# Loads moved to other issuers, repeated products in the last attention steps, and a bias product put last: one change to an attention and feed-forward kernel

## The reference

```python
q = x @ q_w.T + q_b
xd = conv1d(x, conv_w, stride=2, padding=1, groups=C) + conv_b     # 2048 -> 1024 keys
k = xd @ k_w.T + k_b;  v = xd @ v_w.T + v_b
att = softmax(q_heads @ k_heads.T / 4)
y = concat_heads(att @ v_heads) @ out_w.T + out_b
x = layernorm(x + y)
h = layernorm(x) * gamma + beta
w1 = (fc1_q - 128) * scales1;  w2 = (fc2_q - 128) * scales2        # 256 x 1024 and 1024 x 256
z = silu(h @ w1 + fc1_bias) @ w2 + fc2_bias
out = layernorm(x + x + 0.5 * z)
```

## Time and profile of the kernel before

| | us |
|---|---|
| median of 3 runs | 3946.15 |
| lowest, highest | 3940.93, 3949.59 |
| the profiled execution | 3952.87 |
| its span | 3951.1 |

### The profile page before, as it was taken

One profiled execution on the slowest core, in us unless ns is written; L12 is line 12 of the kernel. 1 busy time (PEld: TensorE's weight loads), 2 busy tenths in 40 slices (PEclk: granted clock), 3 DMA queues, 4 the chain that ended last, 5 costly groups with the idle time before them and its releaser, 6 DMA issues. The chain is left out here.

```text
span 3951.1 us, 76505 instructions
## 1 busy us (share of the span) xinstructions
PE 3847.0 (97%) x22696; PEld 1997.0 (51%) x22696; DVE 3336.2 (84%) x4142; ACT 2612.8 (66%) x4968; POOL 840.7 (21%) x547
## 2 busy tenths in 40 slices
PE   9979999999999999999999999999998899999998
PEld 5633333333333333333333333333333799999998
DVE  9968998999899899989989998999995677777775
ACT  4427887878788788878878887878875343343343
POOL 6531000000000000000000000000001687787785
PEclk9979999999999999999999999999997899999999
DMA  8992124105112411510231151133110222222220
GB/s 294 346 207 57 34 38 66 32 29 69 34 33 44 59 34 30 68 37 30 47 56 34 34 70 34 32 50 55 34 56 30 75 86 71 78 85 71 77 85 27
DMA packets 316156, 269.34 MB, mean 68 GB/s; under 512 B 156593, under 2 KB 226225, under 8 KB 316082
## 3 DMA queue, kind: packets, MB, share of 16 engines
q1 hardware_dynamic: 316082, 268.55, 27.9%
HBM read 157.30 MB, written 110.10 MB: 68 GB/s over the span
## 5 line engine op out<-in xcount | busy, mean ns | idle before, releaser
L711 DVE TENSOR_REDUCE half_max<-first_ps 128x2 f32<-128x1024 f32 x2048 | 2413.5, 1221 | 290.8 <-PE first_ps L563 287.1
L679 ACT ACTIVATE probs<-score_ps 128x512 f32<-128x512 f32 x4096 | 2114.9, 603 | 604.0 <-PE score_ps L588 603.4
L588 PE MATMUL score_ps<-q_s,k_s 49*128 49x512 f32 x4096 | 1449.2, 479 | 34.4 <-DMA q_s<-max_row 20.1
L588 PEld LDWEIGHTS score_ps<-q_s,k_s 49*128 49x128 f32 x4096 | 576.7, 186 | 1299.9 <-ACT probs L679 1154.9
L598 PE MATMUL pv_ps<-probs,v_s 128*32 128x512 f32 x8192 | 1109.1, 614 | 0.0
L563 PE MATMUL first_ps<-k_s,q_s 48*128 48x512 f32 x4096 | 912.0, 423 | 26.8 <-PEq L657 18.8
L817 POOL TENSOR_TENSOR num<-num,rden 128x1024 f32<-128x1024 f32 x2 | 4.7, 2356 | 2687.2 <-DMA rden<-rden_d 2687.2
L992 ACT ACTIVATE act_f<-fc_ps,b 128x512 f32<-128x512 f32 x256 | 174.9, 684 | 464.4 <-PE fc_ps L945 462.3
L563 PEld LDWEIGHTS first_ps<-k_s,q_s 48*128 48x128 f32 x4096 | 412.4, 189 | 79.9 <-issue 20.0
L1069 DVE CAST a_hi<-act_f 128x512 fp32r<-128x512 f32 x256 | 243.6, 952 | 146.0 <-ACT act_f L992 144.9
L1121 POOL TENSOR_TENSOR a_lo<-act_f,a_hi 128x512 fp32r<-128x512 f32 x256 | 339.6, 1331 | 86.6 <-DVE a_hi L1069 86.6
(11 more groups left out here) (99 smaller groups left out, 2501.0 us busy)
## 6 DMA issues: line engine op xcount, KB each, us to landing
q_s<-q_hi_d SPq DMA_DIRECT2D x512, 64.0 KB, 2.1
o_d<-o_sb SPq DMA_DIRECT2D x128, 256.0 KB, 2.1
x_t<-x_c_in SPq DMA_DIRECT2D x32, 512.0 KB, 5.7
q_hi_d<-q_hi SPq DMA_DIRECT2D x32, 512.0 KB, 4.7
q_lo_d<-q_lo SPq DMA_DIRECT2D x32, 512.0 KB, 5.1
k_s<-k_hi_d SPq DMA_DIRECT2D x128, 128.0 KB, 4.4
q_s<-q_lo_d SPq DMA_DIRECT2D x256, 64.0 KB, 2.1
x_res<-x_in SPq DMA_DIRECT2D x32, 512.0 KB
```

Of the source, the lines that this page charges most:

```text
L588: pe.matmul(bank(s, u)[:, :], k_s[g][at, a, t * P:(t + 1) * P], q_s[g][at, a, :], start=True, stop=True).then_inc(scored, 1)
L679: nc.scalar.activation(probs[s % 2][:, u, :], bank(s, u)[:, :], ACT.Exp).then_inc(exped, 1)
L711: dve.reduce_max(half_max[g % 2][:, :, a * TT + t, keys], first_ps[keys][:, :, :], AX.X)\
```

## The change

The three loads of each feed-forward weight move to GpSimd's queue: the first behind a wait for the last score of block 0 of attention, the second behind GpSimd's work on the first. SyncE keeps group 1 and the row of maxima at the start of attention; groups 2 and 3 are issued by ScalarE, ahead of its first exponential. In steps 20 to 31 of the last block TensorE computes `again`, two first products of 512 keys twice in a step, in the places where first products stood in earlier steps; nothing reads them, and only the first waits (for VectorE's last reduction). `first_rows` moves two steps ahead. `hidden_bias` comes behind the last step, and the bias sum behind the shift in VectorE's program; the transposes wait for it.

```diff
-def load_w1(sp, e):
+def load_w1(pool, e):
-    sp.dma_start(e["w_int"][:, :, :], e["w1_q"].rearrange("(a p) n -> p a n", p=P)).then_inc(e["w_loaded"], 16)
+    pool.dma_start(e["w_int"][:, :, :], e["w1_q"].rearrange("(a p) n -> p a n", p=P)).then_inc(e["w_loaded"], 16)
     for c in range(CC):
         scales = e["rows"][:, S1_R + c * F:S1_R + (c + 1) * F]
-        sp.dma_start(e["w_s"][:, c, :], scales.to_broadcast([P, F])).then_inc(e["w_loaded"], 16)
+        pool.dma_start(e["w_s"][:, c, :], scales.to_broadcast([P, F])).then_inc(e["w_loaded"], 16)
...
             for j in range(BPB):
                 store(B - 1, j)
-                if j == 0:
-                    load_w1(sp, e)
...
-        ROWS_AT = STEPS - 5
+        ROWS_AT = STEPS - 7
...
-            for g in groups[1:]:
-                load_kv(sp, e, 0, g)
-                load_q(sp, e, 0, g)
-                if g == 1:
-                    load_max(0, 0)
-            sp.wait_ge(w_used, 1)
-            load_w2(sp, e)
+            load_kv(sp, e, 0, 1)
+            load_q(sp, e, 0, 1)
+            load_max(0, 0)
...
+            def again(s, keys):
+
+                if s == STEPS - LEAD and keys == 0:
+                    pe.wait_ge(first_used, FIRSTS + 2)
+                for h in range(2):
+                    at = slice(h * HALF, h * HALF + KROWS)
+                    pe.matmul(first_ps[1][:, h, :], q_s[G - 1][at, 0, 0:P], k_s[G - 1][at, 0, keys * 512:(keys + 1) * 512],
+                              start=True, stop=True)
...
             def first_hidden():
 
-                pe.wait_ge(first_used, FIRSTS + 2)
+                pe.wait_ge(b1_up, 1)
                 pe.wait_ge(hid_up, 1 + TT)
...
                     if ahead:
                         first(n, s + LEAD, 0)
                         first(n, s + LEAD, 1)
+                    else:
+                        again(s, 0)
...
+                    else:
+                        again(s, 1)
...
-                    if not more and s == STEPS - LEAD + 1:
-                        hidden_bias()
...
             one_block(NB - 1, False)
+            hidden_bias()
             first_hidden()
...
+            for g in groups[2:]:
+                load_kv(nc.scalar, e, 0, g)
+                load_q(nc.scalar, e, 0, g)
             act.sem_inc(pv_done, 2)
             exps(0, 0)
...
-            dve.wait_ge(b1_mm, 1)
-            dve.tensor_tensor(b1[:, :], first_ps[1][:, 0, 0:FC], col[:, B1_C:B1_C + FC], ALU.add)
...
                                      op0=ALU.mult, op1=ALU.mult).then_inc(shifted[1], 1)
+            dve.wait_ge(b1_mm, 1)
+            dve.tensor_tensor(b1[:, :], first_ps[1][:, 0, 0:FC], col[:, B1_C:B1_C + FC], ALU.add).then_inc(b1_up, 1)
...
+            pool.wait_ge(scored, 4 * STEPS)
+            load_w1(pool, e)
             pool.wait_ge(w_loaded, 3 * 16)
...
+            load_w2(pool, e)
             pool.wait_ge(w_loaded, 2 * 3 * 16)
```

More of the change, by code:

```diff
@@ L158, in load_rden, with load_w2 @@
         sp.dma_start(e["rden"][j][:, c, :], each_row).then_inc(e["in_loaded"][j], 16)
-def load_w1(sp, e):
-    sp.dma_start(e["w_int"][:, :, :], e["w1_q"].rearrange("(a p) n -> p a n", p=P)).then_inc(e["w_loaded"], 16)
+def load_w1(pool, e):
+    pool.dma_start(e["w_int"][:, :, :], e["w1_q"].rearrange("(a p) n -> p a n", p=P)).then_inc(e["w_loaded"], 16)
     for c in range(CC):
         scales = e["rows"][:, S1_R + c * F:S1_R + (c + 1) * F]
-        sp.dma_start(e["w_s"][:, c, :], scales.to_broadcast([P, F])).then_inc(e["w_loaded"], 16)
-def load_w2(sp, e):
-    sp.dma_start(e["w_int"][:, :, :].rearrange("p c n -> p (c n)").rearrange("p (a n) -> p a n", n=C),
+        pool.dma_start(e["w_s"][:, c, :], scales.to_broadcast([P, F])).then_inc(e["w_loaded"], 16)
+def load_w2(pool, e):
+    pool.dma_start(e["w_int"][:, :, :].rearrange("p c n -> p (c n)").rearrange("p (a n) -> p a n", n=C),
                  e["w2_q"].rearrange("(a p) n -> p a n", p=P)).then_inc(e["w_loaded"], 16)
@@ L459, in attention @@
         begun = sem("sp_begun2")
-        w_up, w_used, b1_mm = sem("w_up"), sem("w_used"), sem("b1_mm")
+        w_up, w_used, b1_mm, b1_up = sem("w_up"), sem("w_used"), sem("b1_mm"), sem("b1_up")
         QL, KVL, ML, OS = 6 * 16, 7 * 16, 2 * 16, 16
```

## The result

The changed kernel takes 3917.17 us, median of 4 runs (3914.98 to 3924.93), beside 3947.56 for the kernel before (4 runs, 3940.93 to 3949.59). The ratio is 0.9932, 95% interval 0.9915 to 0.9948. The prediction was 3916. The profiled execution took 3914.98 us, its span 3913.0.

The account below looks back on a forecast made before the run. Prediction: ScalarE's loop (score, exponential, weighing) sets attention's 2.61 us step; time is lost at the seams into and out of attention. Gains of 7.5 and 22.6 sum to 30.1 us, giving 3916 us from the median; range 3901 to 3928.

Parts of the forecast that it names:

- start: Way into attention: gain from the moved loads, 6.0 to 14.2 us by case, taken as 7.5 us.
- the shared case: Way into attention: groups 1 and 2 share what limits loads; first exponential 3.5 us later, start gain 6.0 us.
- way out: End of attention: full clock through repeats, earlier row products, bias product hidden in idle time; gain 22.6 us.
- First weights out of the projection tail: Projection's end: without weight loads between stores, attention's first product comes 6.2 us earlier, bounds 5.2 and 7.
- Groups 2 and 3 from ScalarE: Attention's start: group 1 22.5 us behind first product, scores at 279.9, ScalarE free at 285.8, first exponential 3.5 us later.
- The stall at 313.57: Ninth step's score: row of maxima goes at once, gaining 8.1 us and 1.4 more from the half-clock step behind.
- rival (c): Seam into feed-forward: clock stays up, 3.7 us more gain, 3912 us; chance 0.10.
- a sign of being wrong: Way out: row products waiting for GpSimd by more than 1 us would show the prediction wrong; 0.2 to 0.4 expected.
- Rival (b): Last steps: clock falls all the same, driven by something other than missing products (the bias product); 3927 us; chance 0.08.
- (a): Way into attention: the two queues don't hinder each other, start gain 14.2 us, 3909 us; chance 0.15.
- (d): Attention's start: ScalarE's 26 issues end past 316 and delay all attention, making it slower; 3960 us at 330; chance 0.02.
- (e): Attention's start: SyncE's loads queue behind ScalarE's, stall moves to first row of maxima; start gain 0, 3923 us; chance 0.08.

Follow-up runs that it names:

- e8: The changed kernel, unchanged, run and profiled once more; 3918.84 us, ratio 0.9925 to the kernel before.
- e2: The changed kernel with the old end: only the new loads (weights from GpSimd, groups 2 and 3 from ScalarE) kept; 3941.67 us, ratio 0.9988.
- e5: The changed kernel with groups 2 and 3 issued by SyncE behind group 1 and the row of maxima, weights still on GpSimd; 3909.96 us, ratio 0.9906.
- e6: The changed kernel with group 2 from ScalarE only once group 1 is down, group 3 from SyncE behind the row of maxima; 3905.93 us, ratio 0.9894.
- e3: The changed kernel without the repeated products, row products early and bias product last kept; 3925.33 us, ratio 0.9944.
- e9: e6 without the repeated products; 3907.17 us, ratio 0.9909.
- e10: e6 unchanged, run again on the chip of e9; 3908.67 us, ratio 0.9907.
- e4: The changed kernel with the bias product back behind step 21 and its sum ahead of the residual, repeats kept; 3927.45 us, ratio 0.9956.
- e11: The kernel before with only the bias product moved behind the last step and its sum behind the shift; 3931.45 us, ratio 0.9966.
- e1: The changed kernel with all loads as before, only the new end kept; 3924.18 us, ratio 0.9946.
- e7: The changed kernel with v loads of groups 2 and 3 at the start in 2 KB rows instead of 64-byte pieces, first batch's sums wrong; 3918.96 us.
- e12: e7 with, in addition, k loads of groups 2 and 3 sent to 128 partitions in 512-byte pieces instead of 16 and 4 KB; 3922.82 us.

## Why the prediction was right, and where not

The time was 3917.17 where 3916 was predicted, and both parts of the sum fit: start 6.1 us (7.5 taken, 6.0 in the shared case), way out 22.7 (22.6 predicted). The way out was added up rightly, with a wrong reason for the clock. The start fits by luck: in it two misses of 1.8 us cancel. And other executions of the same code would have given 1.7 us less at the new end (e8) or 3.9 less at the old one (e2).

**First weights out of the projection tail.** 6.2 predicted, 6.9 measured (254.69 to 247.76), within the bounds of 5.2 to 7.

**Groups 2 and 3 from ScalarE.** The predicted first exponential was 285.8, held by ScalarE's issues, with the scores ready at 279.9. Measured: 287.54, held by the scores, which came at 286.8; ScalarE was free at 281.5. Group 1 came 30.5 us behind the first product, not 22.5. The step that failed is that groups 1 and 2 go down together and group 3 begins behind them, at 271.0. For two groups the time was right: by 270.6 the two queues had moved 2.9 MB (1.69 and 1.21), 22 us after they began, though the 0.33 MB per us for k was read from stores and weights, and alone group 1's loads began at 171 GB/s (e5, 249 to 253). But ScalarE went on to group 3 at 264.33, so that group 1 wasn't down until 278. The second error was ScalarE's issue, 37.8 us predicted and 34.3 measured (247.24 to 281.50): it held nothing up. With scores 6.9 us late and the holder gone, the first exponential is only 1.7 us off. The Trainium skill's page DMA: Bandwidth & Descriptors, section "Issuing engines are not separate DMA queues", has more issuers save issue time alone. The trace agrees, as 30.5 is not 18 and two queues moved 125 GB/s where one moved 123 (e5). It also shows a price: a load that is waited for shares with the others, here for 11 us (e5, e6).

**The stall at 313.57.** It is gone, as predicted, and the step behind it at half clock too. From the first exponential to the tenth step's scores it is 35.2 us before and 23.9 after, 11.3 less where 9.5 was predicted. The rest is the clock of the first steps, which the prediction left out. Before, it rose to full 11.1 us behind the first exponential (granted clock 0.82 over 293 to 294), after only 5.2 behind it (0.62 over 292 to 293). A step at half clock takes 4.07 us (294.18 to 298.25 in e3) instead of 2.61, so 5.9 us less at half are worth 2.1 by estimate. So 1.8 us more were gained here than predicted, and these make good the 1.8 by which the first exponential came later than predicted (5.3 us behind that of before, not 3.5). The other six waits for a row of maxima have 12.0 us in all before (20.1 less 8.1) and 10.1 after, so GpSimd's loads and work in the second block cost nothing that shows. That was taken as 0, with 0 to 4 as bounds.

**The way out.** Steps of 2.67, no more than 0.2 us of wait for the numerators, four row products and three steps, and the bias product hidden: all as predicted, as was the half clock over the seam, against rival (c). The feed-forward stage gained only 1.0 us. The wait for the numerators is not always so short: in e8, the same kernel, it was 1.57 us, above the 1 us that the prediction names as a sign of being wrong.

**The cause of the way out.** Here the prediction was wrong: "The repeats give the last twelve steps the mix of the steps before, at which the clock stood at full". The repeats do nothing in the changed kernel (e3, e9 beside e10). What made the clock fall was the bias product standing among the steps. In the kernel before, e2 and e4 the clock fell within about 1 us of its end (3010.4, 2998.0 and 2996.3), in e4 with the repeats around it. In e3, e9 and e11, with the product last and no repeats, the clock stood at 1.00 through the steps, and fell only at the product. Rival (b) had the right driver, but drew the wrong conclusion: as the change itself moves the product out, the driver leaves with it. I had the evidence in hand: the earlier trace rows has the clock at 0.68 right behind the product, and steps 20 and 21 in the earlier trace rows had no first products and ran at full clock. I used this only for the seam.

**Rivals.** (a) failed by 30.5 us instead of 18. (d), the slow side, did not come near: ScalarE was free at 281.5, not 316. (e) failed: the first product was earlier and the row of maxima in time.

What stays open: what in the bias product makes the clock fall, and what sets the 14.5 to 29.4 us at the changes of batch in single executions.

## What to carry to other kernels

When a change has several parts that aim at one effect, look in the profile for what stood just before the effect began, and run each part alone: here one moved block of 32 small products gave 17.5 of 22.7 us, and the part named as the cause gave nothing. Loads that a program waits for first should have the DMA engines to themselves; a free issuer is worth using only behind them. And compare timelines at fixed marks on both sides of a seam, as single executions here differ by up to 15 us elsewhere.

## What the runs showed of the hardware

- Keeping the clock and getting it back are two things. Steps without first products stayed at 1.00 from the twelfth last to the end (e3, e9, e11). After the fall, the same steps stood at 0.50 for 27 us (e2) and 37.5 us (before), until the first or the third row product; with the repeats the clock was back in 3.4 us (e4).
- The 32 products of one column (3.7 us at full clock, all of it shown as busy) brought a fall of the clock each time, in the middle of dense work (e4) as well as ahead of idleness (after). It came 1.7 (e1) to 4.7 us (after) behind their start, in e1 well before their end, so that they took 5.43 us there.
- Two hardware queues with work in hand moved packets one for one in the stretches read, whatever their size: 526 and 526 with 1.14 and 0.03 MB (e7), 176 and 172 (after), 1839 and 1841 (e12). SyncE's 256 KB in 64-byte pieces landed 8.4 us after issue alone, 17.7 beside ScalarE's queue, and 26.0 when that queue had larger packets (e7). The issuing engine was held 12.64 and 22.67 us in one pair of following loads.
- Two queues were no faster in sum than one, and hardly slower: 117 to 131 GB/s for three groups at once (five executions, 125 in after), 123 one after another (e5), with the engines' share at 1.0 or more. The projection's tail moved stores and weight loads at 337.
